# A two-layer transformer pair on one NeuronCore: the delta rule's triangles stored and loaded group by group, beta's products shared out anew, the last group of the projections in another order

## The reference, cut to what matters

```
q, k, v = silu(causal_conv4(x @ W))           # 128 columns each; then q, k = l2norm
beta, w_global, p = sigmoid(x @ Wb), sigmoid(x @ Wg + bg), softmax(x @ Wl + bl)
A = (k * beta) @ k.T per chunk;  T = inv(eye + tril(A, -1))
u, w = T @ (v * beta), T @ (k * beta)
for each chunk:                               # 32 chunks, one after another
    u = u - w @ S;  o = q @ S + tril(q @ k.T) @ u;  S = S + k.T @ u
local = p0 * v + p1 * causal_conv3(v) + p2 * causal_conv31(v)
o = w_global * o + (1 - w_global) * local;  o = rmsnorm(o) @ Wo
```

## Time and profile before

| | before |
|---|---|
| median of 3 timed runs | 624.46 us (609.24 to 624.79) |
| the profiled execution | 602.81 us, span 601.1 us |
| mean granted TensorE clock | 0.986 of full |
| PE / PEld busy | 546.1 us (91%) / 373.3 us (62%) |
| DVE / ACT / POOL busy | 407.1 (68%) / 324.2 (54%) / 174.4 us (29%) |
| chain that ended last | PE 70%, DVE 13%, ACT 6%, DMA 6% |

### The profile page before, as it was taken

One profiled execution on the slowest core, in us unless ns is written; L12 is line 12 of the kernel. 1 busy time (PEld: TensorE's weight loads), 2 busy tenths in 40 slices (PEclk: granted clock), 3 DMA queues, 4 the chain that ended last, 5 costly groups with the idle time before them and its releaser, 6 DMA issues.

```text
span 601.1 us, 17481 instructions
## 1 busy us (share of the span) xinstructions
PE 546.1 (91%) x7472; PEld 373.3 (62%) x7472; DVE 407.1 (68%) x773; ACT 324.2 (54%) x574; POOL 174.4 (29%) x333
## 2 busy tenths in 40 slices
PE   4799999999999999999999996996999779897993
PEld 2445555555555557777777785774667667565672
DVE  5697999999999826263545337345899871576774
ACT  2327888788888876655555645556422330125441
POOL 7000111445535422010101006246982560010101
PEclk9899999999999999999999999898999999999998
DMA  4778667374240000001000000021673300000011
GB/s 118 153 224 212 190 149 147 81 154 79 57 104 7 5 2 2 0 7 31 1 2 1 0 1 0 2 36 39 124 93 73 73 4 4 5 1 1 1 36 35
DMA packets 54051, 33.82 MB, mean 56 GB/s; under 512 B 38853, under 2 KB 45509, under 8 KB 53974
## 3 DMA queue, kind: packets, MB, share of 16 engines
q1 hardware_dynamic: 48822, 31.65, 23.8%
q10 hardware_dynamic: 5152, 1.05, 1.1%
HBM read 20.83 MB, written 9.44 MB: 50 GB/s over the span
## 4 chain that ended last, share of the span: by engine, by line
PE 70%; DVE 13%; ACT 6%; DMA 6%; issue 2%; SPq 1%; POOL 1%; POOLq 0%; ACTq 0%; DVEq 0%
PE ps L1760 10%; PE ps L1745 9%; PE ps L1512 7%; PE ps L1514 6%; PE ps L1513 6%; PE ps L1860 6%; DMA qst<-shift_sb 4%; PE ps L1724 3%; PE ps L1933 2%; PE ps L2065 2%; DVE filtered L1344 2%; PE ps L2066 2%; ACT prob L682 2%; PE ps L1926 2%; PE ps L1602 1%
## 5 line engine op out<-in xcount | busy, mean ns | idle before, releaser
L1203 DVE TENSOR_REDUCE nmx<-ps 128x1 f32<-128x1024 f32 x128 | 154.1, 1218 | 16.6 <-PE ps L1725 15.2
L682 ACT ACTIVATE prob<-ps 128x512 f32<-128x512 f32 x256 | 137.4, 597 | 26.6 <-PE ps L1745 26.1
L1760 PE MATMUL ps<-prob,vp 128*32 128x128 f32 x2048 | 78.9, 278 | 0.0
L1745 PE MATMUL ps<-qst,kst 50*128 50x512 f32 x256 | 73.6, 492 | 4.7 <-ACT prob L682 3.5
L1760 PEld LDWEIGHTS ps<-prob,vp 128*32 128x32 f32 x2048 | 49.2, 109 | 39.8 <-ACT prob L682 22.4
L1076 DVE TENSOR_TENSOR h_lo<-hf,h_hi 128x512 fp32r<-128x512 f32 x48 | 33.1, 690 | 52.4 <-ACT h_hi L591 50.2
L1512 PE MATMUL ps<-h_hi,w_lo 128*128 128x512 f32 x144 | 58.1, 403 | 2.4 <-DVE h_lo L1076 2.4
L1514 PE MATMUL ps<-h_hi,w_hi 128*128 128x512 f32 x144 | 57.0, 396 | 0.0
L1513 PE MATMUL ps<-h_lo,w_hi 128*128 128x512 f32 x144 | 56.9, 395 | 0.0
L1724 PE MATMUL ps<-kst,qst 48*128 48x512 f32 x128 | 52.6, 412 | 2.2 <-DMA kst<-k_scratch 1.6
L1725 PE MATMUL ps<-kst,qst 48*128 48x512 f32 x128 | 51.5, 404 | 0.0
(11 more groups left out here) (248 smaller groups left out, 1102.3 us busy)
## 6 DMA issues: line engine op xcount, KB each, us to landing
qst<-q_scratch SPq DMA_DIRECT2D x31, 192.0 KB, 4.5
kst<-k_scratch SPq DMA_DIRECT2D x31, 192.0 KB, 4.8
w_raw<-L_ffn_h_w SPq DMA_DIRECT2D x8, 256.0 KB, 3.9
kd<-ka SPq DMA_DIRECT2D x8, 256.0 KB, 6.5
X<-L_attn_x SPq DMA_DIRECT2D x4, 256.0 KB, 5.0
qst<-shift_sb SPq DMA_DIRECT2D x64, 4.0 KB
q_scratch<-w_hi SPq DMA_DIRECT2D x2, 512.0 KB, 5.0
k_scratch<-w_lo SPq DMA_DIRECT2D x2, 512.0 KB, 3.3
```

Source lines behind the costliest of these rows:

```text
L682: nc.scalar.activation(prob[:, n % PROBS, GT * (t % 2):GT * (t % 2) + GT], ps[:, RINGB + i % RING, :], ACT.Exp, scale=SCORE_SCALE).then_in ...
L1203: nc.vector.tensor_reduce(nmx[:, u % 2, j:j + 1], pair, AX.X, ALU.max, negate=True).then_inc(max_done, 1)
L1745: nc.tensor.matmul(ps[:, RINGB + i % RING, :], kst[r:r + 50, p, P * t:P * t + P], half_of(qst[r:r + 50, p, :], u % 2), start=True, stop=Tr ...
L1760: last = nc.tensor.matmul(ps[32 * j:32 * j + 32, PVB, P * half:P * half + P], vp[:, h, t, :], prob[:, n % PROBS, c:c + P], start=(t == 0), ...
```

## The change

The triangles of a batch row are stored and loaded in two halves k, one group each, and the DRAM layouts have the group outermost. The load of a half fills 64 partitions. GpSimd multiplies the triangles of groups 0 and 1 by beta ahead of v and k. VectorE does the triangles of groups 2 and 3 where they are masked, and v and k of group 2 just ahead of its inverse; v and k of group 3 go to GpSimd, behind the inverse of b = 0. Group 3 is projected as v, q, k, its chunk products go to banks 0 to 3, and the 3-tap filter runs before them. `split_x(2)` is ahead of a normalisation, and the clearing that starts VectorE's inverse comes a group later. `begin_outputs(0, ...)` stands before `times_inverse(1)`, products that keep TensorE busy there change their number and bank, and GpSimd's eight additions stand behind `g_ready` of b = 1. The PSUM banks of the transition products (`MG_BANK`) and of the state's inputs (`B_BANK`) change for that.

```diff
-    FIR_BANK, UW_BANK, MG_BANK, B_BANK = (0, 4), (4, 0), (0, 4), (4, 0)
+    FIR_BANK, UW_BANK, MG_BANK, B_BANK = (0, 4), (4, 0), (0, 0), (6, 6)
+    KTOK_BANK, TRI_BANK = (0, 0, 0, 4), (4, 4, 4, 0)
+    KQV_ORDER = ((0, 1, 2), (0, 1, 2), (0, 1, 2), (2, 1, 0))
+
+    def nth_conv(g, i):
+        return 3 * g + KQV_ORDER[g].index(i) + 1
+
+    def nth_norm(g, i):
+        return 2 * g + (i if g < GROUPS - 1 else 1 - i) + 1
...
-                sp.wait_ge(low_ready[b], 2)
-                for h in range(4):
-                    sp.dma_start(low_dram[b, h].rearrange("n c t e -> (c t) n e"), low[:, h, 8 * b:8 * b + 8, :]).then_inc(low_stored[b], 16)
-                sp.wait_ge(low_stored[b], 64)
-                sp.dma_start(lp[:, b], low_dram[b].rearrange("h n c t e -> (h n c) t e")).then_inc(low_in[b], 16)
+                for k in range(2):
+                    t = 8 * b + 4 * k
+                    sp.wait_ge(low_ready[b], k + 1)
+                    for h in range(4):
+                        sp.dma_start(low_dram[b, k, h].rearrange("n c t e -> (c t) n e"), low[:, h, t:t + 4, :]).then_inc(low_stored[b], 16)
+                    sp.wait_ge(low_stored[b], 64 * k + 64)
+                    sp.dma_start(lp[64 * k:64 * k + 64, b], low_dram[b, k].rearrange("h n c t e -> (h n c) t e")).then_inc(low_in[b], 16)
...
-            eng.wait_ge(low_in[b], 16)
+            eng.wait_ge(low_in[b], 32)
...
+            silu(GROUPS - 1, 2)
+            vtok_copy(GROUPS - 2)
+            silu(GROUPS - 1, 1)
+            ktok_copy(GROUPS - 2)
+            silu(GROUPS - 1, 0)
+            nc.scalar.preload_act_table_set("natural_log_exp_and_others")
+            norms(GROUPS - 1, 1)
+            norms(GROUPS - 1, 0)
+            vtok_copy(GROUPS - 1)
+            gate_exps(GROUPS - 1)
...
             copy_filtered(1)
+            copy_filtered_tokens(1)
+            act.wait_ge(tT_zeroed, 1)
+            clear_keys(0)
+            ktok_copy(GROUPS - 1)
             clear_keys(1)
-            copy_filtered_tokens(1)
...
+                triangles_times_beta(nc.gpsimd, pool, g)
                 times_beta(nc.gpsimd, pool, g)
-                triangles_times_beta(nc.gpsimd, pool, g)
...
+            pool.wait_ge(beta_ready, GROUPS)
+            times_beta(nc.gpsimd, pool, GROUPS - 1)
+            pool.wait_ge(vb_ready[1], 2)
...
+            pool.wait_ge(uw_psum, B)
+            nc.gpsimd.memset(state[:, 0], 0.0).then_inc(state_zeroed, 1)
+            pool.wait_ge(g_ready, 2)
             for i, g in enumerate(FINAL):
-                if i == 2:
-                    pool.wait_ge(uw_psum, B)
-                    nc.gpsimd.memset(state[:, 0], 0.0).then_inc(state_zeroed, 1)
-                    pool.wait_ge(g_ready, 2)
...
+            split_x(2)
             normalise_rows2(GROUPS - 1, rstd2_ready, x2_ready, mv2, rs2)
             normalise(0, 1)
-            start_inverse(nc.vector, link, 1)
-            for g in range(1, GROUPS):
+            for g in range(1, GROUPS - 1):
                 gate_logits(g)
-                if g + 1 < GROUPS:
+                if g >= 2:
                     split_x(g + 1)
                 square(g, 0)
                 square(g, 1)
                 if g == 1:
                     dve.wait_ge(masks_ready, 1)
                 masks(g - 1)
-                if g >= 3:
-                    triangles_times_beta(nc.vector, dve, g - 1)
-                    times_beta(nc.vector, dve, g - 1)
+                if g == 2:
+                    start_inverse(nc.vector, link, 1)
                 gate_sigmoids(g)
                 normalise(g, 0)
                 normalise(g, 1)
-            masks(3)
-            triangles_times_beta(nc.vector, dve, 3)
-            times_beta(nc.vector, dve, 3)
+            gate_logits(GROUPS - 1)
+            square(GROUPS - 1, 1)
+            masks(GROUPS - 2)
+            triangles_times_beta(nc.vector, dve, GROUPS - 2)
+            square(GROUPS - 1, 0)
+            normalise(GROUPS - 1, 1)
+            normalise(GROUPS - 1, 0)
+            gate_sigmoids(GROUPS - 1)
+            masks(GROUPS - 1)
+            triangles_times_beta(nc.vector, dve, GROUPS - 1)
...
+            times_beta(nc.vector, dve, GROUPS - 2)
             invert(nc.vector, dve, link, 1)
...
+            conv(GROUPS - 1, 2)
+            gate_products(GROUPS - 1)
+            v_to_tokens(GROUPS - 2)
+            conv(GROUPS - 1, 1)
+            triangles(GROUPS - 2)
+            k_to_tokens(GROUPS - 2)
+            conv(GROUPS - 1, 0)
+            sums(GROUPS - 1, 1)
             v_to_tokens(GROUPS - 1)
+            pe.wait_ge(diag_ready, 1)
+            pe.wait_ge(tri_masked, GROUPS - 1)
+            pe.wait_ge(att_ready, GROUPS - 1)
+            filter_values(1, (0,))
+            sums(GROUPS - 1, 0)
...
+            filter_values(1, (1, 2)).then_inc(fir_psum, 1)
...
             triangles(GROUPS - 1)
...
+            filtered_to_tokens(1)
+            pe.wait_ge(att_ready, GROUPS)
+            filter_values(0, range(4))
...
             k_to_tokens(GROUPS - 1)
...
+            filter_values(0, range(4, FIRL)).then_inc(fir_psum, 1)
...
-            keep_busy(7, 5)
+            keep_busy(5, 5)
             inputs_of_state(0)
-            keep_busy(7, 8)
+            keep_busy(5, 3)
             pe.wait_ge(m_ready, 1)
             pe.wait_ge(g_ready, 1)
+            for n in range(4):
+                begin_outputs(0, n)
             times_inverse(1)
             pe.wait_ge(b_ready, 1)
             transition_products(1)
-            keep_busy(3, 5)
+            keep_busy(7, 6)
             inputs_of_state(1)
-            keep_busy(3, 2)
-            pe.wait_ge(m_ready, 2)
-            pe.wait_ge(g_ready, 2)
-            for n in range(4):
-                begin_outputs(0, n)
```

More of the change, by code:

```diff
@@ L705, in _, with silu @@
                     gated_hi(g + 1)
-            for g in range(GROUPS):
-                for i in range(3):
-                    act.wait_ge(conv_psum, 3 * g + i + 1)
-                    dst = (rows(ks, g), rows(qs, g), v_rows(g))[i]
-                    nc.scalar.activation(dst, ps[:, (1, 2, 1)[i], :], ACT.Silu).then_inc(silu_done, 1)
-                    if i == 0 and g == 0:
-                        scale_y2(GROUPS - 1)
-                    if i == 0 and g + 1 < GROUPS:
-                        load_x(g + 1)
-                    if i == 1 and g >= 1:
-                        vtok_copy(g - 1)
+            def silu(g, i):
+                act.wait_ge(conv_psum, nth_conv(g, i))
+                dst = (rows(ks, g), rows(qs, g), v_rows(g))[i]
+                nc.scalar.activation(dst, ps[:, (1, 2, 1)[i], :], ACT.Silu).then_inc(silu_done, 1)
+            for g in range(GROUPS - 1):
+                silu(g, 0)
+                if g == 0:
+                    scale_y2(GROUPS - 1)
+                load_x(g + 1)
+                silu(g, 1)
+                if g >= 1:
+                    vtok_copy(g - 1)
+                silu(g, 2)
                 if g >= 1:
@@ L1590, in conv @@
             def conv(g, i):
[L1592 removed]
+                if i != 1 and i == KQV_ORDER[g][0] and g >= 1:
                     pe.wait_ge(silu_done, 3 * g)
```

123 lines of the change are left out of this document (61 added, 62 removed).

## The result

The changed kernel takes **613.11 us** (median of 20 runs, 608.23 to 629.6), the kernel before 604.27 (20 runs, 601.33 to 624.79). The ratio is 1.0144, 95% interval 1.0115 to 1.0173: 1.4% slower, inside 2% and of the wrong sign; I had forecast 5.9 us less. The absolute number, 618.5, was near only because the three runs shown had a median 20 us above the later one. The granted clock differs between executions of one kernel: where runs of the kernel before took 600 to 606 us it was 0.974 to 0.989 of full over the span, where they took 620 to 627 us, the level on which two of the first three lie, 0.924 to 0.945. All 20 runs of the changed kernel had 0.950 or less.

What follows compares the result with a forecast made beforehand. Bound: the chain to the scan's start, ending in VectorE's queue, with the inverse's chain just behind. Terms -1.1 - 1.3 - 1.4 + 1.6 - 3.5 - 0.2 = -5.9 us gave 618.5 us from the median 624.46; range 600 to 624.

Steps and rivals of the forecast that it cites:

- the slower rival: Scan, steps 1 to 30: clock falls to half before it and stays; +12 us, net +6, 630.5 us; chance 0.05.
- step 7: Before `times_inverse(1)`: `begin_outputs(0)` moves into TensorE's wait there; -0.2 us, bounds 0 and -2.05.
- Step 1: `split_x(2)` placed earlier, ahead of a normalisation, where TensorE stood idle 4.65 us; -1.1 us, bounds 0 and -4.65.
- step 2: Group 3 as v, q, k before its chunk products: -0.8 from order, -0.5 from clock; sum -1.3 us, bounds 0 and -2.5.
- 3.: Half-sized stores and load, beta products to VectorE's inverse: -1.4 us; about -0.7 if only the stores get shorter.
- 4.: `times_beta` moved: group 2's products replace group 3's on VectorE before its inverse; cost nothing, up to 0.8 us.
- 5.: VectorE's inverse: less overlap with GpSimd's inverse -0.6, GpSimd's eight products +2.2; sum +1.6 us, bounds -2 and +4.
- 6.: VectorE's queue behind the weighings: additions moved away free it before u and w are copied; -3.5 us, bounds 0 and -3.5.

Runs made afterwards that it cites:

- c1_fill3: Changed kernel with 3 full-sized filling products on TensorE before the wait for the state's zeroes, ahead of the scan; 603.31 us.
- b1_entry: Kernel before with only the entry to the scan changed: `begin_outputs(0)` before `times_inverse(1)`, its banks and `keep_busy` numbers; 618.72 us, ratio 1.0293.
- a1_fill: Changed kernel with eight products whose results nothing reads in TensorE's wait right before the scan; 594.97 us, ratio 0.9886 to the kernel before.
- c2_burst: Changed kernel with 16 full-sized products in place of 1 at step 4 of the scan; 602.64 us, ratio 0.9909.
- c3_rows: a1_fill with triangles stored and loaded in whole rows and the inverse's old DRAM layout, as in the kernel before; 599.24 us, ratio 0.9899.
- d2_add_back: a1_fill with GpSimd's first two groups of additions back ahead of its wait for the second batch's placing; 597.63 us, ratio 0.987.
- b2_hole: Kernel before with four clearings of a dead tile on VectorE before the scan's first state, so TensorE waits there; 623.7 us, ratio 1.0373.
- e1_again: a1_fill unchanged, run again against the kernel before; 594.24 us, ratio 0.9857.
- d3_more: a1_fill with 6 full-sized products in place of 3 before `begin_outputs(0)`, in the wait for the second batch's inverse; 595.9 us.
- c4_entry_fill: b1_entry with 8 full-sized products before the wait for the state's zeroes; 603.41 us, ratio 0.999 to the kernel before.
- d1_hole_burst: b2_hole with 16 full-sized products in place of 1 at step 8 of the scan; 620.15 us, ratio 1.0222 to the kernel before.
- a2_begin_back: Changed kernel with `begin_outputs(0)` back behind `inputs_of_state(1)` and eight `keep_busy` products behind the inputs of b = 0; 615.65 us.

## Why the prediction was wrong

The step that failed is **the slower rival's threshold**: "It decides from the point where TensorE's last wait before step 1 reaches some 4 us", with "I count 1.5 to 2 us of wait" against it. On these grounds the sum left the scan as long as it was; it grew by 15.7 us. Both numbers were wrong. The wait was 2.65 us; c1_fill3's profiled execution lost the clock behind one of 1.78 us, and b1_entry's behind 1.89. I had named the mechanism, place and sign, and gave it 0.05. The limit of 4 us came from the earlier trace rows, one idle of 4.15 us that was followed by half clock and one of 1.96 that was not: two points in front of other work. The chance deserved to be much larger, because step 7 took away two full-sized products and the 64 of `begin_outputs` right in front of a stretch that then runs 50 us on small tiles. That the time still fell inside my range is luck: the range was wide for the median's two levels and meant to leave this rival out. Its price was nearly right: 54.4 - 38.7 = 15.7 us for 12.

Of the wait, my count missed 0.7 to 1.2 us: from the copy of u to the first state product it took 484.05 - 477.01 = 7.04 us for my 6.2. The copy of the state, for which I had taken 0.9, took 1.24: it began inside one of GpSimd's additions and ended 0.06 us after it. So it went in eight profiled executions, this one among them, and each time the copy ended 0.05 to 0.06 us behind the addition; where it began at the end of an addition, as in a1_fill and c2_burst, it took 0.20.

The steps, up to the scan's start:

1. and 2. The beta products end at 418.65 + 1.96 = 420.61 for 422.05: -1.4 for both, where I summed -2.4. TensorE's row of group 3's chunk products, below, stands at 415.93 for 417.02: -1.1. Step 1 had given 1.3 us at group 1's chunk products (376.31 for 377.60), but only 0.45 of it was left at group 3's gate logits (400.99 for 401.44), so the other 0.6 is step 2's new order. The products took 1.48 us for 1.97, the -0.5 that I took for the clock; VectorE's product with beta behind them took 0.14 more.

```profile
415.93 1.48 PE L1701 MATMUL ps<-kq 32*32 32x64 f32 x128 [0.20 <-DVE kq L1130]
```

3. -0.8 for -1.4 in this execution: 428.27 - 420.61 = 7.66 us for 8.46. The load took 428.27 - 424.69 = 3.58 us as against 3.57 with half the bytes. That is what I had written would mean half the term. The Trainium skill (SBUF — State Buffer, section "Door 1: The DMA port swizzle") has each half of the partitions, 0 to 63 and 64 to 127, on half of the ports; the load timed here goes to the upper half. The trace agrees with it, and so does c3_rows (3.97 with halves, 3.45 with whole rows), but a load whose time hardly depends on its bytes would look the same, and no run tells the two apart. The -0.7 lies nearer to this execution's -0.8; over the other executions even that is not steady, since four of them took 10.0 to 10.6 us for this stretch.
4. Nothing, as I had said: idle of 1.35 us was left before the inverse.
5. Wrong sign: 462.75 - 428.27 = 34.5 us for 35.8; I had 37.4. GpSimd's eight products cost VectorE almost nothing: beside them (449 to 454 us) its products of 252 elements took 0.62 and 0.46 us, and 0.62 and 0.42 in the kernel before with GpSimd idle. What is left is the shorter overlap with GpSimd's inverse, 447.40 - 428.27 = 19.1 us for 453.96 - 430.51 = 23.4; that the gain comes from it is argued, no run isolates it. It made 2.9 us against my sum.
6. -3.4 for -3.5: from `times_inverse(1)` to the copy of u 477.01 - 470.93 = 6.08 us, before 485.95 - 476.45 = 9.50. d2_add_back's rows show the cause.
7. For the scan's start +0.7 for -0.2; for the time the loss.

In addition the inverse's way through DRAM, which I had left unchanged, took 470.93 - 462.75 = 8.18 us for 476.45 - 466.35 = 10.10. In c3_rows, with the old layout, it was 472.20 - 463.39 = 8.81, so the layout may be 0.6 of the 1.9, by one execution; the rest wasn't settled. The sum: -1.4 - 0.8 - 1.3 - 1.9 - 3.4 + 0.7 = -8.1, for -8.3 measured.

**What stays open:** why one execution keeps the clock and the next of the same kernel does not. Part of it is that the waits themselves differ, as c2_burst shows; the rest is unexplained. The share changes with the waits: none of 20 runs kept the clock in the changed kernel and none of 8 in b1_entry and b2_hole, two of four in c1_fill3, all ten of a1_fill and e1_again (0.981 or more over the span). But the other kernels with the same filling did lose it at times: one of four in d3_more, two of twelve in c4_entry_fill (609.46 and 610.67 us, the latter within the scan), and in c3_rows the profiled one for a part of the scan and two more of ten (606.24 us, and one of 723.46, whose granted clock of 0.658 nothing explains). The kernel before loses it too, in 9 of the 26 runs taken with c4_entry_fill (0.959 or less). What is shown is that a wait put right before the scan brings the fall (b2_hole) and that filling it keeps the clock at the scan's start (a1_fill); how waits further ahead and small products count together isn't.

## What to carry over

Before a long stretch of small TensorE products, count TensorE's waits as a cost of the whole stretch, not as idle off the path: a cut of 8.3 us turned into a loss of 7.4 since some microseconds of waiting set the speed of the next 50. Whoever moves work out of the place ahead of such a stretch puts filling products in (they make the fall rarer, not impossible), and prices a clock's fall by the stretch's length and not by the wait. Compare the granted clock run by run before a median of three is taken as the level.

## What the hardware showed that I had not expected

- The scan's small tiles (32 and 64 columns, with one of 512 in most steps) never brought the clock back: it stayed at 0.50 for 51 us with TensorE busy nearly throughout. Sixteen products of 128x512 did, some 2 us after the first of them began (d1_hole_burst). Other small tiles did as well: within the 128 products of 64 columns of `times_inverse(1)` the clock came back from 0.50 at about 475 us in a2_begin_back and 477.5 in e1_again. What sets the two apart isn't shown.
- The scan's tiles don't hold a full clock safely either: in c3_rows, c4_entry_fill and d3_more it fell among them with no wait above 0.7 us near.
- Waits further ahead act too: in b1_entry the clock fell behind one of 1.89 us, before the wait of 2.56 began.
- At half clock a step of the scan grew from 1.27 us (a1_fill) to 2.08 while `begin_outputs` fills it (485.79 to 487.87 in the changed kernel).
- VectorE's copy of 128x64, 0.20 us long, took up to 1.26 when it began inside one of GpSimd's additions of 128x512: it ended 0.05 to 0.06 us after the addition, in eight profiled executions. The scan's additions on VectorE (0.23 us) were not held so.
- GpSimd's additions slowed VectorE's weighings of 128x512 (11.60 for 8.38 us for eight), but its products of 128x128 hardly VectorE's inverse (at most 0.04 us a product).
